# VectorE as a second engine for exponentials: two of 50 key tiles also in units six to eight of a decoder layer's cross-attention, and lanes scored where TensorE's next group leaves a row tile free

## What is computed

```python
q = (query @ Wq + bq).reshape(B, Nq, H, D).transpose(0, 2, 1, 3)
k = (key_value @ Wk + bk).reshape(B, Nkv, H, D).transpose(0, 2, 1, 3)
v = (key_value @ Wv + bv).reshape(B, Nkv, H, D).transpose(0, 2, 1, 3)
attn = jnp.einsum('bhqd,bhkd->bhqk', q, k) * scale
attn = jax.nn.softmax(attn, axis=-1)
x = jnp.einsum('bhqk,bhkd->bqhd', attn, v).reshape(B, Nq, Cq)
```

## Time and profile before

| | us |
|---|---|
| median of three runs | 946.25 |
| lowest, highest | 946.11, 951.87 |
| the profiled execution, its own time | 945.66 |
| its span, first to last instruction | 942.5 |
| ACT busy, of the span | 841.0 (89%) |
| PE busy, of the span | 868.7 (92%) |
| DVE busy, of the span | 373.2 (40%) |

### The profile page before, as it was taken

How to read it: one execution, slowest core, us unless ns; L and a number is a source line. 1 busy time by engine, 2 the same in 40 slices (tenths; PEclk the granted TensorE clock), 3 DMA queues, 4 the chain that set the end, 5 groups by cost and what they waited for, 6 DMA issues and landing times.

```text
span 942.5 us, 15734 instructions
## 1 busy us (share of the span) xinstructions
PE 868.7 (92%) x6269; PEld 274.7 (29%) x6269; DVE 373.2 (40%) x789; ACT 841.0 (89%) x702; POOL 46.7 (5%) x104
## 2 busy tenths in 40 slices
PE   6977888998899999999999999999999999998997
PEld 4562222222222222222222232232222322222543
DVE  5765644331499469929972120110010001000432
ACT  5667987999999999999999999999999999998432
POOL 4000000000000000000000013000000000010300
PEclk9998999999999999999999999999999999999999
DMA  4253004711121111122112214223333210110120
GB/s 150 97 201 59 1 1 129 233 35 34 37 38 34 34 37 39 41 56 41 37 34 38 37 40 138 37 59 57 57 60 59 59 55 34 56 63 15 36 100 13
DMA packets 24812, 56.14 MB, mean 60 GB/s; under 512 B 6986, under 2 KB 12084, under 8 KB 24476
## 3 DMA queue, kind: packets, MB, share of 16 engines
q1 hardware_dynamic: 21276, 44.18, 19.0%
q0 software_dynamic: 3456, 10.88, 4.0%
HBM read 37.59 MB, written 9.59 MB: 50 GB/s over the span
## 4 chain that ended last, share of the span: by engine, by line
PE 45%; ACT 27%; DVE 14%; issue 12%; DMA 1%; SPq 0%; ACTq 0%; DVEq 0%
ACT probs L862 27%; PE psum L1685 18%; PE psum L1649 10%; PE psum L1980 3%; PE psum L1988 3%; DVE kparts_bc L1153 2%; DVE w_quads L1153 2%; DVE attnT L1142 2%; DVE attnT L1143 2%; PE psum L1923 2%; PE psum L1518 1%; PE psum L1558 1%; PE psum L1562 1%; PE psum L1805 1%; DVE attnT L1147 1%
## 5 line engine op out<-in xcount | busy, mean ns | idle before, releaser
L862 ACT ACTIVATE probs<-psum 128x1536 f32<-128x1536 f32 x570 | 773.6, 1512 | 28.4 <-PE psum L1649 14.2
L1685 PE MATMUL psum<-probs,v_ctx 128*9 128x512 f32 x3128 | 409.3, 595 | 2.7 <-DVE turned L1100 2.4
L1649 PE MATMUL psum<-q_all,k_ring 32*128 32x512 f32 (+1 forms) x1756 | 290.3, 487 | 44.3 <-ACT probs L862 40.6
L1649 PEld LDWEIGHTS psum<-q_all,k_ring 32*128 32x128 f32 x1756 | 111.9, 183 | 429.2 <-ACT probs L862 389.0
L1685 PEld LDWEIGHTS psum<-probs,v_ctx 128*9 128x9 f32 x3128 | 46.5, 88 | 102.2 <-issue 96.5
L1100 DVE STREAM_TRANSPOSE turned<-psum 128x512 f32<-128x512 f32 x16 | 11.5, 717 | 135.2 <-PE psum L1681 120.1
L933 ACT ACTIVATE probs<-psum,b_sb 128x512 f32<-128x512 f32 x32 | 22.0, 687 | 33.8 <-PE psum L1980 33.8
L1153 DVE SCALAR_TENSOR_TENSOR kparts_bc<-kparts_bc,attnT 128x512 f32<-128x512 f32 x60 | 41.5, 692 | 2.0
L1685 PE MATMUL psum<-probs,v_self 128*9 128x512 f32 (+3 forms) x384 | 40.3, 519 | 1.8 <-DVE probs L1121 1.2
L1416 DVE COPY kparts_bc<-psum 128x128 f32<-128x128 f32 x11 | 3.2, 292 | 96.5 <-PE psum L1923 96.5
L739 POOL DMA_INDIRECT block_rows<-xn,slots x8 | 7.9, 984 | 549.0 <-DVE slots L1387 546.8
(11 more groups left out here) (227 smaller groups left out, 555.7 us busy)
## 6 DMA issues: line engine op xcount, KB each, us to landing
k_ring<-kc_parts SPq DMA_DIRECT2D x256, 52.0 KB
k_ring<-kc_parts SPq DMA_DIRECT2D x256, 48.0 KB
kc_parts<-kparts_bc SPq DMA_DIRECT2D x8, 512.0 KB, 2.8
q_all<-w_region POOLq DMA_DIRECT2D x13, 256.0 KB, 3.6
q_all<-ctx_region POOLq DMA_DIRECT2D x13, 256.0 KB, 4.1
kc_parts<-probs SPq DMA_DIRECT2D x4, 512.0 KB, 3.5
w_region<-in_L_ffn_W SPq DMA_DIRECT2D x1, 2048.0 KB, 9.9
probs<-gate_rows SPq DMA_DIRECT2D x2, 1024.0 KB, 5.7
```

The costliest lines, as they stand in the source:

```text
L862: act.activation(probs[:, slot:slot + w, :], psum[:, at:at + w, :], ACT.Exp, scale=SC[ph]).then_inc(L[ph]["exp_done"], 1)
L1649: mm = pe.matmul(into[:, col:col + n_q], keys, q_all[rows, g, hf * HALF + q0:hf * HALF + q0 + n_q], start=True, stop=True)
L1685: mm = pe.matmul(into[:, q0:q0 + w], v_all[:, h, t, :], probs[:, place(ph, at)[1], col:col + w], start=first, stop=last)
```

## The change

Three things move. (1) `VECTOR_OF` replaces the two tables: units 1, 2 and 3 keep three tiles for DVE, now 15, 30 and 45, and units 5, 6 and 7 give it tiles 30 and 45. (2) `vector_plan` places each lane at a group whose number fits lane r (r = -at mod 4, the row tile that score group at + 3, the next one that PE makes, leaves out), at least five groups from the lane before it, not next to a side job, and not in a unit's last group or the five ahead of it; a tile's sum stands at the next number that divides by four and is free, or at the group before the unit's end. (3) Waits on the side bank (`side_free`) count lanes and jobs together, and the tiles of units 5 to 7 have two sets of four buffers of their own, in space that is out of use.

By this plan ACT's cross groups go from 522 to 514, and the units' ends to 66, 129, 191, 254, 321, 385, 449 and 513. Lanes stand at 67, 72, ..., 122 (unit 1), 130 to 185 (unit 2), 192 to 247 (unit 3), then at 297, 302, 307, 328, 334, 343, 352, 361 (unit 5's eight, the first three of them while PE is in unit 4), 366 to 433 (unit 6) and 438 to 505 (unit 7). Sums stand at 88, 108, 128, 152, 172, 190, 212, 232, 252, and for the new tiles at 336, 368, 408, 440, 480, 512. The side jobs keep their numbers.

```diff
--- before.py
+++ after.py
@@ -61,8 +61,8 @@
 POWERS = (-753.2122192382812, 522.0867309570312, -180.93753051757812, 41.80864715576172, -7.287735462188721)
 
 
-VECTOR_TILES = (3, 15, 40)
-VECTOR_UNITS = (1, 2, 3)
+VECTOR_TILES = (15, 30, 45)
+VECTOR_OF = {1: (15, 30, 45), 2: (15, 30, 45), 3: (15, 30, 45), 5: (30, 45), 6: (30, 45), 7: (30, 45)}
...
@@ -128,7 +128,7 @@
     for half in range(NHALF):
         for g in range(QUADS):
             for t in range(KT):
-                if half * QUADS + g in VECTOR_UNITS and t in VECTOR_TILES:
+                if t in VECTOR_OF.get(half * QUADS + g, ()):
                     continue
...
@@ -252,17 +252,36 @@
 B2_AT, COUNT_AT, TURN_AT, HIDDEN_AT = (SUMMED_AT - SUMMED_AT % 4 + n for n in (36, 40, 60, 80))
 BLOCK_STEP, OUTPUT_STEP = 16, 8
 
-
-VECTOR_LANES, VECTOR_SUMS = {}, {}
-for _unit in VECTOR_UNITS:
-    _half, _g = _unit // QUADS, _unit % QUADS
-    _before = unit_ends(1)[_unit - 1][3]
-    for _n, _t in enumerate(VECTOR_TILES):
-        for _r in range(LANES):
-            _at = -(-(_before - 2) // 4) * 4 + 4 * (LANES * _n + _r)
-            VECTOR_LANES[_at] = (_unit, _g, _half, _t, _r)
-        VECTOR_SUMS[_at + 8] = (_unit, _g, _half, _t)
-    assert _at + 8 < unit_ends(1)[_unit][3]
+SIDE_WORK = (list(range(SUMMED_AT + 1, COUNT_AT + 4)) + [TURN_AT + 4 * q for q in range(-(-BLOCKS // 4))] +
+             [HIDDEN_AT + BLOCK_STEP * j + n for j in range(EARLY) for n in (0, OUTPUT_STEP)])
+
+
+def vector_plan():
+
+
+
+    lanes, sums, number, ends = {}, {}, 0, [e[3] for e in unit_ends(1)]
+    for unit, tiles in VECTOR_OF.items():
+        at = ends[unit - 1] + 1 if unit < QUADS else max(lanes) + 1
+        for t in tiles:
+            left = set(range(LANES))
+            while left:
+                r = -at % 4
+                if (r in left and not {at - 1, at, at + 1} & set(SIDE_WORK) and not any(at <= e <= at + 5 for e in ends)
+                        and not any(at - 4 <= n for n in lanes)):
+                    lanes[at] = (number, unit % QUADS, unit // QUADS, t, r)
+                    left.remove(r)
+                at += 1
+            last = max(lanes)
+            at = next((n for n in range(last + 5, ends[unit]) if n % 4 == 0 and n not in SIDE_WORK), ends[unit] - 1)
+            assert last + 5 <= at
+            sums[at] = (number, unit % QUADS, unit // QUADS, t)
+            at = last + 1
+            number += 1
+    return lanes, sums
+
+
+VECTOR_LANES, VECTOR_SUMS = vector_plan()
 
...
@@ -376,7 +395,16 @@
 
...
         vector_p = ([kparts_bc[:, n // 2, n % 2, :] for n in range(LANES)],
-                    [w_space[:, r * HALF:(r + 1) * HALF] for r in range(3)] + [v_space[:, 0:HALF]])
+                    [w_space[:, r * HALF:(r + 1) * HALF] for r in range(3)] + [v_space[:, 0:HALF]],
+                    [w_space[:, 2 * HALF:3 * HALF], v_space[:, 0:HALF], v_space[:, HALF:2 * HALF],
+                     heads[:, 0:HALF // 32, :, :].rearrange("p c g d -> p (c g d)")],
+                    [xnT[:, 0:HALF], xnT[:, HALF:2 * HALF],
+                     xn[:, 0:4, :].rearrange("p b d -> p (b d)"), ctx_region[:, E * NF * D:E * NF * D + HALF]])
+        FIRST_TILES = sum(len(VECTOR_OF.get(unit, ())) for unit in range(QUADS))
+
+        def vector_weights(n):
+
+            return vector_p[n % 2 if n < FIRST_TILES else 2 + (n - FIRST_TILES) % 2]
...
@@ -1128,9 +1156,10 @@
                             beside[group]()
                 steps, lanes_made = [0], [0]
 
-                def vector_lane(n, r):
-
-                    lane = n * LANES + r
+                def vector_lane(at):
+
+                    n, _, _, _, r = VECTOR_LANES[at]
+                    lane = sorted(VECTOR_LANES).index(at)
 
...
@@ -1147,7 +1176,7 @@
                     step_of_lane(dve.tensor_scalar(vector_n.bitcast(I32), vector_n, 127.0 - ROUND, 2.0 ** 23, ALU.add, ALU.mult))
                     if n >= 2:
                         dve.wait_ge(s["vector_summed"], n - 1)
-                    weights = vector_p[n % 2][r]
+                    weights = vector_weights(n)[r]
                     step_of_lane(dve.scalar_tensor_tensor(weights, vector_u, POWERS[4], vector_u, ALU.add, ALU.mult))
...
@@ -1162,14 +1191,17 @@
                     step(ins)
 
                 while n < len(ends):
-                    if ph == 1 and n in VECTOR_UNITS:
-                        for i in range(len(VECTOR_TILES)):
-                            for r in range(LANES):
-                                vector_lane(VECTOR_UNITS.index(n) * len(VECTOR_TILES) + i, r)
+                    if ph == 1 and n < QUADS:
+                        for group in sorted(VECTOR_LANES):
+                            if n and ends[n - 1][3] <= group < ends[n][3]:
+                                vector_lane(group)
                     if ph == 1 and n >= QUADS:
-                        for group in sorted(block_work):
+                        for group in sorted([*block_work, *VECTOR_LANES]):
                             if ends[n - 1][3] <= group < ends[n][3]:
-                                block_work[group]()
+                                if group in block_work:
+                                    block_work[group]()
+                                else:
+                                    vector_lane(group)
...
@@ -1608,27 +1640,41 @@
                     norms_of_ctx(range((c - 2) * CHUNK, (c - 1) * CHUNK), c - 1)
             norms_of_ctx(range((NCHUNK - 2) * CHUNK, KT + 1), NCHUNK).then_inc(s["norms_ctx"], 1)
 
+
+            with_lanes = [True]
+
+            def side_free(at):
+
+                lanes = sum(n < at for n in VECTOR_LANES)
+                if lanes and with_lanes[0]:
+                    pe.wait_ge(s["vector_taken"], lanes)
+                done = [("output" if n else "hidden", j) for j in range(EARLY) for n in (0, OUTPUT_STEP)
+                        if HIDDEN_AT + BLOCK_STEP * j + n < at] or \
+                    [("turned", q) for q in range(-(-BLOCKS // 4)) if TURN_AT + 4 * q < at]
+                if done:
+                    pe.wait_ge(s["block_done"], block_step(*done[-1]))
+                elif at > COUNT_AT:
+                    pe.wait_ge(s["block_done"], block_step("counts"))
+
             def vector_scores(at):
                 _, g, hf, t, r = VECTOR_LANES[at]
                 load = load_of(hf, g, t)
                 slot, t0 = load % PIECE_RING, PIECES[piece_of(t)][0]
                 rows = slice(ROWS * r, ROWS * r + ROWS)
                 lane = sorted(VECTOR_LANES).index(at)
-                if r == 0:
+                if True:
                     pe.wait_ge(s[f"k_loaded{slot}"], 16 * LANES * COPIES * (load // PIECE_RING + 1))
-                if lane:
-                    pe.wait_ge(s["vector_taken"], lane)
+                side_free(at)
                 keys = slot * PIECE + (t - t0) * P
                 pe.matmul(bank(SIDE_BANK), k_ring[rows, keys:keys + P], q_all[rows, g, hf * HALF:(hf + 1) * HALF],
                           start=True, stop=True).then_inc(s["vector_ps"], 1)
 
             def vector_sums(at):
-                _, g, hf, t = VECTOR_SUMS[at]
-                n = sorted(VECTOR_SUMS).index(at)
+                n, g, hf, t = VECTOR_SUMS[at]
                 pe.wait_ge(s["vector_made"], LANES * (n + 1))
                 for r in range(LANES):
                     mm = pe.matmul(bank(OUT_BANK)[ROWS * r:ROWS * r + VC, :], vector_v[:, LANES * g + r, VECTOR_TILES.index(t), :],
-                                   vector_p[n % 2][r], start=False, stop=False)
+                                   vector_weights(n)[r], start=False, stop=False)
                 mm.then_inc(s["vector_summed"], 1)
 
...
@@ -1903,8 +1949,7 @@
 
             def turn_block_rows(q):
                 pe.wait_ge(s["rows_moved"], ROWS_LOADED)
-                if q:
-                    pe.wait_ge(s["block_done"], block_step("turned", q - 1))
+                side_free(TURN_AT + 4 * q)
...
@@ -1925,14 +1970,11 @@
                 mm.then_inc(s["block_ps"], 1)
 
             def early_hidden(j):
-                if j:
-                    pe.wait_ge(s["block_done"], block_step("output", j - 1))
-                else:
-                    pe.wait_ge(s["block_done"], block_step("turned", -(-BLOCKS // 4) - 1))
+                side_free(HIDDEN_AT + BLOCK_STEP * j)
                 hidden_of_block(j, bank(SIDE_BANK))
 
             def early_output(j):
-                pe.wait_ge(s["block_done"], block_step("hidden", j))
+                side_free(HIDDEN_AT + BLOCK_STEP * j + OUTPUT_STEP)
                 output_of_block(j, bank(SIDE_BANK)[:, 0:D])
 
...
@@ -1957,6 +1999,7 @@
                 first_routed[HIDDEN_AT + BLOCK_STEP * j + OUTPUT_STEP] = lambda j=j: early_output(j)
 
             def general_cross():
+                with_lanes[0] = False
 
                 for r in range(LANES):
                     pe.matmul(bank(OUT_BANK)[ROWS * r:ROWS * r + VC, :], v_ctx[:, r, KT, :], ptail[:, 0:HALF],
```

## The result

The change takes 940.8 us (median of six runs, 937.8 to 941.7) against 947.1 beside it (six runs, 945.1 to 951.9): ratio 0.9924, 95% interval 0.9897 to 0.9952. The forecast was 939.8, a gain of 6.5; the medians differ by 6.3.

A forecast was written before the change was run, and what follows sets the result against it. ACT was taken as the saturated bound at 1.344 us per group, with PE close behind. Terms -10.75 - 2.2 + 3.0 + 2.0 + 0.6 + 0.5 + 0.3 gave -6.5: 939.8 us median, range 934.5 to 943.5.

The forecast's parts named there:

- (a): Six tiles leave ACT's groups: 8 groups at 1.344, 10.75 us gained if ACT stays the bound.
- (b): Units 1 to 3: lanes every five groups end PE's waits for DVE and the array clash; 2.2 us gained.
- (e): Sums at 128, 190 and 252, close to the ends of units 1 to 3: 2.0 us lost together.
- (c): The 24 lane matmuls in units 5 to 7, in the free row tile: taken as 0, bounds 0 and 0.43 each.
- Its rival: Lane matmul behind a sum runs alone in units 5 to 7: 10.3 us lost, 950.1 in all; chance 0.08.
- (d): DVE tiles' sums fill empty bare groups; PE's lateness 1.23 exceeds ACT's cover 0.63: 0.60 per sum, 3.0 us lost.
- (g): Lanes 366 and 478, two groups behind a hidden job: PE waits about half a us for DVE; 0.3 lost for both.
- The last sum: The sum at 512, ahead of the short one-bank last group, leaves 0.5 us on the path into the rest.
- (f): Behind the ends of units 4 to 6 PE recovers more slowly, bare groups being taken: 0.2 each, 0.6 us lost.
- The larger cover: Rival: ACT's cover against late PE is larger, so the new sums are hidden; 935.5 us, chance 0.15.
- the 3 to 9 that I had named: Sign: the forecast is wrong if ACT's lost time in units 5 to 7 is below 3 or over 9 us.
- POOL starved while DVE works: Rival: unit 5's first lanes delay POOL's row transfers, PE waits at group 312; 3.0 us lost, 942.8, chance 0.12.

The follow-up runs named there:

- Experiment 2: The new tiles of units 5 to 7 as in the change, but lanes of units 1 to 3 at every fourth group as before; ratio to before 0.9922.
- experiment 3: The changed kernel with PE leaving out the six sums of DVE's tiles in units 5 to 7, lanes kept; ratio to before 0.9886.
- experiment 4: The changed kernel with every lane in a row tile that the next group uses; ratio to before 0.9999.

## Why the prediction was right

By its own steps:

- (a) and the pace, right: 514 cross groups, ACT the bound, bare pitch 1.343.
- (b), right in size, wrong in its reason: the waits for DVE are gone and unit 1 gained 1.5 (forecast 1.7; 85.83 against 85.7). But I had put them down to lanes of 5.54 at every four groups of 5.38. Experiment 2 keeps that spacing, and the clash with it, has no wait for DVE either and takes 85.63. It is the first lane's place behind the unit's end that ends the waits, which the new placing brings along; that the sum came out is in this part luck. In the changed kernel a lane there waits for nobody, and it is DVE that waits for its lane, 1.85 at this one:

```profile
267.62 0.69 DVE L1171 TENSOR_SCALAR attnT<-psum 128x512 f32<-128x512 f32 x1 [1.85 <-PE psum L1669]
```

- (e), right: units 1 to 3 were forecast at -2.2 + 2.0 with (b) and came to -0.2 (257.03 against 257.25). Against experiment 2, ACT's exponentials around the three ends are later by 0.4 (groups 126 to 140), 0.9 (187 to 200) and 0.6 (248 to 262), 1.9 in all, forecast 0.3, 1.0 and 0.6. Unit 2's end shows it, with the sum at 190 (420.01) in a group that has one already, and 2.27 from one score row to the next (forecast 2.39):

```profile
418.71 0.50 PE L1695 MATMUL psum<-q_all,k_ring 32*128 32x512 f32 x3
419.15 1.05 PE L1731 MATMUL psum<-probs,v_ctx 128*9 128x512 f32 x8
420.01 0.60 PE L1676 MATMUL psum<-w_quads,v_gen 128*9 128x512 f32 x3
...
420.98 0.50 PE L1695 MATMUL psum<-q_all,k_ring 32*128 32x512 f32 x3
```

- (c), right: a lane behind a sum is free, 0.43 at 620.00. Its rival, for which the forecast had 950.1 and which decides from 0.27 per lane, is out by experiment 3; experiment 4 shows that the condition is the row tile.
- (d), right in place and size: 0.60 behind the sum at 336, as worked out from a cover of 0.63 and a peak of 1.23. Behind the five sums it is 0.60, 0.82, 0.61, 0.60 and 0.77, 3.4 in all; the two larger ones follow the lanes 366 and 478 and hold what (g) had put down. (d) and (g) were 3.3.
- (g), right in place, smaller in size: PE waits 0.2 for DVE at lanes 366 and 478, not half a us, and in experiment 3, without the sums, the exponentials around each come about 0.1 later, 0.2 for both (forecast 0.3).
- The last sum: from the third exponential from the end to unit 7's transpose it is 5.92 in the change and 5.48 in experiment 3, so 0.44, forecast 0.5. The five sums ahead of it then make the other 3.1 of experiment 3's 3.55, forecast 3.0.
- (f), near in size, but not where it was put. Eight groups are 10.75, experiment 3 gains 9.99, and 0.76 is left. (g) has 0.2 of it. The end of unit 5 has the rest: over the fifteen groups behind it ACT loses 1.33 in experiment 3, and 0.78 before the change, where one idle of 0.32 stands at that end and not two of 0.18 and 0.43. The ends of units 4 and 6 cost what they did (over the same fifteen groups 0.99 and 1.36 in experiment 3, 1.05 and 1.23 before), where the forecast had 0.2 more for each. And in experiment 3 no sum takes a bare group, so that was not the reason. The end now falls at group 385 instead of 387; what of this costs the 0.55 is open.
- The larger cover is out: the sums are not hidden, and ACT's loss over the bare pitch in units 5 to 7 went from some 2.5 to 6.8, within the 3 to 9 that I had named.
- POOL starved while DVE works: the contention is there, its price is not. POOL's transfers from 570 us on, beside a lane, in the changed kernel:

```profile
570.17 0.96 POOL L767 DMA_INDIRECT block_rows<-xn,slots  x1 [0.30 <-issue]
571.44 1.48 POOL L767 DMA_INDIRECT block_rows<-xn,slots  x1 [0.31 <-issue]
573.22 1.14 POOL L767 DMA_INDIRECT block_rows<-xn,slots  x1 [0.30 <-issue]
574.67 0.96 POOL L767 DMA_INDIRECT block_rows<-xn,slots  x1 [0.30 <-issue]
```

  Two transfers are 0.5 and 0.2 longer. In all seven profiles of kernels with the new tiles two of the last three transfers take 1.02 to 1.48, and in the seven without them none does. The rival had each of six wait 0.69, 4.2 in all. From the first transfer to POOL's going on it is 22.6 us instead of 22.0, and PE turns the rows at 588.32, straight behind its scores of 587.89.

- Not forecast: unit 4's 0.8, the stop before group 302. Without unit 4 the stretch is 6.7 shorter, and the forecast was 6.5. The agreement of the medians (6.3) rests on times that hold such a stop or not, so it says less than the terms do.

## What to carry to other kernels

When work is handed to an idle engine, ask what the busy engine next to the bound still has to do for it: here PE's sums, 0.98 each, took back a third of the eight groups. Work the busy engine's lateness out group by group against its cover, and put extra sums where it has time to recover: some 0.6 each was lost in a bare group, and 0.9 for the sum beside another one at a unit's end. If the idle engine's pace is only a little short of its schedule, look first at when it may start: lanes placed behind a unit's end took away all waits at the old spacing. And in this kernel a matmul on a quarter of the array is free where the matmuls beside it leave its row tile out, and 0.21 us where they don't; over 60 lanes that was 4.2 us by the stages, and by the ratios the whole 0.8%.
